# Probabilities turned by a bounce through DRAM, with ctx's blocks in four transfers, other PSUM banks and orders, and buffers on 512 bytes

## The chip, the cores and the metric

One core of one Trainium2 chip runs the whole program. The metric is the device time of the program in microseconds; the span of the profile, from the first instruction to the last, is some 2 us shorter. The kernel before was run three times: median 3147.73 us, 3147.18 to 3148.7.

## The reference, cut to what matters

64 items of 128 x 512 pass through two blocks. Block L0 is an attention over 512 positions with 128 channels and 1x1 convolutions; block L1 is a 16-head cross attention (head width 32, 128 queries, 128 keys) with an MLP of width 2048. All is float32.

```
# L0: x and ctx are (64, 128, 512); Wn, Wm, Wl, Wo are 128 x 128
Mn = Wn @ inorm(x) + bn ;  Mm = Wm @ inorm(ctx) + bm
A  = softmax(Mn^T Mm)                      # 512 x 512 for each item
x1 = Wo @ ((Wl @ ctx + bl) @ A^T) + bo + x
# L1
q = layer_norm(x1) @ q_w ; k = ctx @ k_w ; v = ctx @ v_w     # 16 heads of 32, biases left out here
attn = softmax(where(mask, q k^T / sqrt(32), min))
hidden = (attn @ v) @ cproj_w + cproj_b + x1
out = hidden + gelu(layer_norm(hidden) @ fc_w + fc_b) @ proj_w + proj_b
```

## The kernel before

The program is two passes. **attention_pass** computes `hidden` item by item and stores it in DRAM; **mlp_pass** reads it in 16 groups of four items and writes `out`. Float32 precision on TensorE comes from three passes: each operand is split into a high half of type float32r and the low rest, and a product is a_hi b_lo + a_lo b_hi + a_hi b_hi (`three_passes`). So each split operand needs a ScalarE or VectorE copy (hi) and a subtraction (lo).

In the first pass one item goes through five pipeline stages, one per **slot**. In slot s, b0 = item s does M, the 512 x 512 scores S0 and their exp into A; b1 = s-1 turns A (AT), computes u, x1 and k and v; b2 = s-2 normalises x1, computes q, the head scores S1, their row maxima (line 798) and the exps (line 618) into `probs`; b3 = s-3 normalises the probabilities on GpSimd (line 510), turns them on TensorE (line 936, 16 transposes of 128 x 128, evicted to `pT` on ScalarE, line 605), multiplies with v (PV, line 951), splits outT and starts cproj; b4 adds the residual into `hid` (line 700), which is stored. Slots 6 and on are a hardware loop of two slots (`slots`, `Item`). Each engine runs its own list of instructions strictly in the order written in its `slot` function and waits on semaphores; there is no planner. The orders of the five lists therefore set everything. All DMAs are issued by SyncE, whose `slot` stores hidden of b4, loads x and ctx of item s+2, the residual x and the mask, and then ctx's blocks for item s+1.

ctx is turned without TensorE: `load_blocks` brings the 32 x 32 blocks of an item into transposed block places in 16 transfers of 16 KB in pieces of 128 bytes, and one VectorE transpose (line 791), which turns each 32 x 32 block within itself, finishes the job. VectorE also scales A by the reciprocal sums (line 751) and makes the high halves of the normed inputs (line 778). The second pass turns its activations in the same manner, from SBUF into SBUF (`spread`, line 1096, and line 1220), for all groups but the first.

All SBUF tensors are allocated in the order of the code. `ident` fills 512 bytes of each partition and `neghalf` 16, so `stage`, `rows`, `y`, `first_hi` and `first_lo` behind them start 160 bytes past a multiple of 512. `rest_hi` and all that follows in the second pass starts 448 past one, and so do qc_hi, qc_lo and outT; ctxT, m and normed start 32 past, xnT 256 past. The split weights of k and v, and the first two weight stages of the MLP, share `first_hi` and `first_lo`.

## Time and profile before

| | |
|---|---|
| profiled execution | 3145.55 us, span 3143.7 us |
| median of the runs shown | 3147.73 us |
| first pass | to about 1724 us, 26.0 us an item in its loop |
| second pass | from about 1725 us, 16 groups |
| granted TensorE clock, mean | 0.994 |
| DMA packets | 342,417, of them 286,176 under 512 bytes |
| HBM | read 97.57 MB, written 33.55 MB |

The page gives each engine's busy time as a sum over the span. A matmul's duration in the trace overlaps the next one's: in a steady stream a long matmul (512 columns) lasts about 390 ns in the record while the next starts about 230 ns after it. The busy column is therefore the union of all.

### The profile page before, as it was taken

The numbers are of one execution on the slowest core, as the hardware profiler recorded it, in microseconds if no ns is written. First come the engines' busy times: TensorE is split into PE (matmuls) and PEld (weight loads), VectorE is DVE, ScalarE is ACT, GpSimd is POOL, SyncE is SP. The second block draws the span as 40 slices with busy tenths as digits, with TensorE's granted clock in tenths as the row PEclk, the third lists the DMA queues.
The fourth block names the chain that finished last, engine by engine and source line by source line (L and its number), as shares of the span: only waits on it lengthen the run. The fifth ranks groups of instructions, "written<-read, shape, count | busy, mean of one in ns | idle before, by whom it ended". The sixth has DMA issues, their size and how long they took to land. (4 is left out here: it accounts for less than half of the span.)

```text
span 3143.7 us, 56992 instructions
## 1 busy us (share of the span) xinstructions
PE 3091.3 (98%) x18551; PEld 2556.6 (81%) x18551; DVE 1952.3 (62%) x3961; ACT 1353.6 (43%) x3954; POOL 818.0 (26%) x742
## 2 busy tenths in 40 slices
PE   7999999999999999999997999999999999999999
PEld 5888888888888888888886788888888888888887
DVE  7888888888888888888885533333333333333332
ACT  4666666666666666666665311111111111111111
POOL 4444444444444444444443100000000000000000
PEclk9999999999999999999998999999999999999999
DMA  4111111111111111111112311111111111111110
GB/s 116 49 51 50 50 50 50 50 50 51 53 51 54 51 52 53 50 50 50 50 37 67 97 32 41 40 40 40 40 33 20 40 33 34 40 40 40 40 27 14
DMA packets 342417, 147.59 MB, mean 47 GB/s; under 512 B 286176, under 2 KB 286688, under 8 KB 342368
## 3 DMA queue, kind: packets, MB, share of 16 engines
q1 hardware_dynamic: 342368, 146.96, 17.6%
q8 instruction: 28, 0.46, 0.1%
q14 instruction: 21, 0.17, 0.0%
HBM read 97.57 MB, written 33.55 MB: 42 GB/s over the span
## 5 line engine op out<-in xcount | busy, mean ns | idle before, releaser
L1163 ACT ACTIVATE gl<-pre,fc_bias 128x512 f32<-128x512 f32 x256 | 176.6, 690 | 1127.9 <-PE pre L1248 1127.9
L1202 DVE CAST hT_hi<-gl 128x512 fp32r<-128x512 f32 x256 | 108.9, 426 | 847.5 <-ACT gl L1163 847.5
L618 ACT ACTIVATE rows<-bank,negmax 128x128 f32<-128x128 f32 x1024 | 362.9, 404 | 89.4 <-DVE negmax L798 89.4
L1247 PE MATMUL pre<-yT_hi,rest_lo 128*128 128x512 f32 x768 | 299.2, 390 | 0.0
L1246 PE MATMUL pre<-yT_lo,rest_hi 128*128 128x512 f32 x768 | 299.0, 389 | 0.0
L1248 PE MATMUL acc<-rest_hi,hT_hi 128*128 128x512 f32 x768 | 298.9, 389 | 0.0
L1248 PE MATMUL pre<-yT_hi,rest_hi 128*128 128x512 f32 x768 | 298.8, 389 | 0.0
L1246 PE MATMUL acc<-rest_lo,hT_hi 128*128 128x512 f32 x768 | 298.8, 389 | 0.0
L1247 PE MATMUL acc<-rest_hi,hT_lo 128*128 128x512 f32 x768 | 298.8, 389 | 0.0
L510 POOL TENSOR_TENSOR rows<-rows,rsum 128x512 f32<-128x512 f32 x256 | 258.8, 1042 | 18.8 <-DVE rsum L693 18.8
L862 PEld LDWEIGHTS bank<-ident,rows 128*128 128x128 f32 x2048 | 234.1, 142 | 22.4 <-ACT rows L618 3.7
L862 PE MATMUL bank<-ident,rows 128*128 128x128 f32 x2048 | 247.1, 274 | 4.2 <-ACT rows L618 3.3
L618 ACT ACTIVATION_READ_ACCUMULATOR rows<-bank,negmax 128x1 f32 x1024 | 249.2, 243 | 0.0
L154 POOL TENSOR_TENSOR rstd<-ve,neghalf 128x4 f32<-128x4 f32 x16 | 16.3, 1019 | 888.3 <-DVE ve L148 888.3
L589 ACT ACTIVATE rows<-bank,negmax 128x512 f32<-128x512 f32 x256 | 173.5, 685 | 122.7 <-DVE negmax L721 122.7
L831 PE MATMUL bank<-first_lo,ctxT_hi 128*128 128x512 f32 x512 | 214.1, 418 | 0.0
L833 PE MATMUL bank<-first_hi,ctxT_hi 128*128 128x512 f32 x512 | 203.0, 397 | 0.0
L832 PE MATMUL bank<-first_hi,ctxT_lo 128*128 128x512 f32 x512 | 202.5, 395 | 0.0
L535 POOL TENSOR_TENSOR normed_lo<-normed,normed_hi 128x512 fp32r<-128x512 f32 x128 | 180.4, 1431 | 50.1 <-DVE normed_hi L778 50.1
L1204 DVE TENSOR_TENSOR hT_lo<-gl,hT_hi 128x512 fp32r<-128x512 f32 x256 | 177.3, 693 | 8.8
L1246 PEld LDWEIGHTS pre<-yT_lo,rest_hi 128*128 128x128 f32 x768 | 144.2, 188 | 30.5
L1248 PEld LDWEIGHTS pre<-yT_hi,rest_hi 128*128 128x128 f32 x768 | 144.2, 188 | 30.3
(158 smaller groups left out, 7277.8 us busy)
## 6 DMA issues: line engine op xcount, KB each, us to landing
x_in<-in_x SPq DMA_DIRECT2D x64, 256.0 KB, 2.7
ctx_in<-in_ctx SPq DMA_DIRECT2D x64, 256.0 KB, 2.9
blocks<-in_ctx SPq DMA_DIRECT2D x1024, 16.0 KB, 2.0
small<-in_x SPq DMA_DIRECT2D x64, 256.0 KB, 3.3
hidden<-hid SPq DMA_DIRECT2D x64, 256.0 KB, 2.1
rows<-hidden SPq DMA_DIRECT2D x16, 1024.0 KB, 5.6
out<-rows SPq DMA_DIRECT2D x64, 256.0 KB, 2.1
stage<-y SPq DMA_DIRECT2D x240, 64.0 KB, 2.3
```

The lines of the kernel that those rows point to most:

```text
L510: pool.tensor_tensor(probs[:, r, :, :], probs[:, r, :, :], rsum1[:, r, :].unsqueeze(2).to_broadcast([P, 4, P]), ALU.mult).then_inc(probs_s ...
L535: pool.tensor_tensor(normed_lo[:, i, :], normed[:, i, :], normed_hi[:, i, :].bitcast(F32), ALU.subtract).then_inc(normed_lo_set, 1)
L618: act.activation(probs[:, r, c, :], by_chunk(S1_BANK[r])[:, c, :], ACT.Exp, bias=negmax1[:, r, c:c + 1], accum_out=sum1[:, r, c:c + 1]).th ...
L831: pe.matmul(out, a_hi, b_lo, start=first, stop=False)
L832: pe.matmul(out, a_lo, b_hi, start=False, stop=False)
L833: return pe.matmul(out, a_hi, b_hi, start=False, stop=last)
L862: last = pe.transpose(out[:, c * P:(c + 1) * P], src(c), ident[:])
L1163: act.activation(gl[:, i % 2, :], pre[i % 2][:], ACT.Gelu_apprx_tanh, bias=mlp.fc_bias[:, i:i + 1]).then_inc(gelu_done, 1)
L1204: dve.tensor_tensor(hT_lo[:, i % 2, :], gl[:, i % 2, :], hT_hi[:, i % 2, :].bitcast(F32), ALU.subtract).then_inc(hT_lo_set, 1)
L1246: pe.matmul(out, a_hi, b_lo, start=first, stop=False)
L1247: pe.matmul(out, a_lo, b_hi, start=False, stop=False)
L1248: return pe.matmul(out, a_hi, b_hi, start=False, stop=last)
```

## The change

- The probabilities are no longer turned on TensorE. GpSimd normalises them one slot earlier (for b2, in four pieces between other work). At the start of the next slot SyncE writes them to a DRAM scratch `p_turn` in four transfers, whose source is in pieces of 32 elements (`write_probs`), and reads them back in four transfers of 32 partitions each with rows of 2 KB (`read_probs`) into `p_blocks`, which lies in the weights' staging buffer. Four VectorE transposes of 32 x 32 blocks then write `pT`. The ScalarE evictions (line 605) and the 16 TensorE turns (line 936) are gone.
- ctx's blocks come in four transfers with 512-byte pieces in place of 16, and VectorE turns them with strided access patterns, earlier in its slot. The resulting order of ctx's columns is permuted. It is matched by the order in which the k and v weights are staged and by a permuted column order in which the exp writes A.
- ScalarE takes over the scaling of A and the high halves of the normed inputs.
- PSUM banks are assigned anew, and the orders on all engines change: cproj of an item is computed one slot later, behind M; TensorE does the head scores before PV, and PV waits for the VectorE turns; the k turn comes before V. VectorE adds `hid` after m_lo.
- Small tensors are allocated first with a pad or last, so that all large buffers start on multiples of 512 bytes.
- The MLP's weight stages swap halves of the staging buffer (`half_of`), and its second stage is loaded two slots later.

```diff
+        sb("pad", [P, PAD])
...
+        p_blocks = stage[:, 0, :, :]
+        p_turn = nc.dram_tensor("p_turn", [4, P, T], F32, kind="Internal").ap()
...
-        M_BANK = (5, 6)
-        AT_BANK = (4, 0, 1, 7)
...
+        M_BANK = (4, 7)
+        C_BANK = PV_BANK = 5
+        AT_BANK = S1_BANK = (0, 1, 2, 3)
...
# SyncE
-                    for c in range(4):
-                        sp.dma_start(to[32 * d:32 * (d + 1), :, c, :], of[:, :, c, d, :]).then_inc(blocks_in, 16)
+                    sp.dma_start(to[32 * d:32 * (d + 1), :, :], of[:, :, d * P:(d + 1) * P]).then_inc(blocks_in, 16)
...
+            def write_probs(e):
+                after(probs_set, e.nth(4, 4))
+                for d in range(4):
+                    sp.dma_start(p_turn[d].rearrange("p (h b) -> p h b", b=32),
+                                 mlp.rows[:, 1, :, :].rearrange("p r (c d b) -> p d (r c) b", d=4, b=32)[:, d])\
+                      .then_inc(p_written, 16)
+
+            def read_probs(e):
+                if e.has_before(1):
+                    after(pT_set, (e + -1).nth(4, 4))
...
+                after(p_written, e.nth(64, 64))
+                for d in range(4):
+                    sp.dma_start(p_blocks[32 * d:32 * (d + 1), :, :],
+                                 p_turn[d].rearrange("(q p) n -> p q n", p=32)).then_inc(p_blocks_in, 16)
+
             def slot(s):
-                e = s + -4
-                if e.exists():
-                    after(hid_set, e.nth(1, 1))
-                    sp.dma_start(hidden[e.number], hid[:, e.parity, :]).then_inc(hid_stored[e.parity], 16)
+                if (s + -3).exists():
+                    write_probs(s + -3)
...
+                e = s + -4
+                if e.exists():
+                    after(hid_set, e.nth(1, 1))
+                    sp.dma_start(hidden[e.number], hid[:, e.parity, :]).then_inc(hid_stored[e.parity], 16)
+                if (s + -3).exists():
+                    read_probs(s + -3)
...
# GpSimd
+                normalise(0)
+                normalise(1)
                 if b0.exists():
                     pool.wait_ge(ctxT_hi_set, b0.nth(1, 1))
...
+                normalise(2)
+                normalise(3)
# ScalarE
-                if b3.exists():
-                    for r in range(4):
-                        act.wait_ge(pT_turned, b3.nth(4, r + 1))
-                        act.activation(pT[:, r, :, :].rearrange("p c n -> p (c n)"), bank[PT_BANK[r]][:],
-                                       ACT.Copy).then_inc(pT_copied, 1)
+                if b0.exists():
+                    act.wait_ge(rsum0_set, b0.nth(1, 1))
+                    for t in range(DC):
+                        act.activation(A[:, t, :], A[:, t, :], ACT.Identity,
+                                       scale=rsum0[:, t:t + 1]).then_inc(a_scaled, 1)
...
+                if ahead.exists():
+                    for i in range(2):
+                        act.wait_ge(normed_set, ahead.nth(2, i + 1))
+                        act.activation(normed_hi[:, i, :], normed[:, i, :], ACT.Copy).then_inc(normed_hi_set, 1)
...
+                if b2.exists() and b2.has_before(1):
+                    act.wait_ge(p_written, b3.nth(64, 64))
                 exp1(0)
                 exp1(1)
+                if b3.exists():
+                    act.wait_ge(outT_done, b3.nth(1, 1))
+                    act.activation(flat(outT_hi), bank[PV_BANK][:], ACT.Copy).then_inc(outT_hi_set, 1)
+                exp1(2)
...
                 exp1(3)
# VectorE, behind qT and x1n
-                if b3.exists():
-                    dve.wait_ge(outT_hi_set, b3.nth(1, 1))
-                    lower(flat(outT_lo), bank[PV_BANK][:], flat(outT_hi), outT_lo_set)
+                if b3.exists():
+                    dve.wait_ge(p_blocks_in, b3.nth(64, 64))
+                    for r in range(4):
+                        dve.transpose(pT[:, r, :, :].rearrange("p c (q b) -> p c q b", b=32),
+                                      p_blocks[:, :, r * P:(r + 1) * P].rearrange("p q (c b) -> p c q b", b=32))\
+                           .then_inc(pT_set, 1)
                 if b2.exists():
                     dve.wait_ge(s1_done, b2.nth(1, 1))
...
# TensorE; S1, ahead of this, stood behind PV
+                if b3.exists():
+                    pe.wait_ge(pT_set, b3.nth(4, 4))
...
```

## Rows read from the trace of the kernel before

**Rows 1.** The page, part 1: busy us (share of the span) and instructions, by engine.

```profile
PE 3091.3 (98%) x18551; PEld 2556.6 (81%) x18551; DVE 1952.3 (62%) x3961; ACT 1353.6 (43%) x3954; POOL 818.0 (26%) x742
```

**Rows 2.** Stages, window by window: columns PE, PEld, DVE, ACT, POOL, PEclk, DMA share, GB/s.

```profile
500.00:1000.00 500.00, 500.00 (x3694) 416.92 (x3694) 425.95 (x888) 330.17 (x1074) 206.73 (x191) 1.00 0.19 51
```

**Rows 3.** Timeline of PE in one slot: start, us, engine, line, operation, tiles, count.

```profile
1000.00 1.91 PE L862 MATMUL bank<-ident,rows 128*128 128x128 f32 x16
1001.74 0.60 PE L862 MATMUL bank<-ident,x1n 128*128 128x128 f32 x4
...
1005.07 1.08 PE L951 MATMUL bank<-y,v_sb 128*32 128x128 f32 x32
...
1007.30 0.50 PE L831 MATMUL bank<-first_lo,ctxT_hi 128*128 128x512 f32 x1
...
1025.77 0.39 PE L833 MATMUL bank<-u_hi,small_hi 128*128 128x512 f32 x1
```

**Rows 4.** Groups by line, second pass: after the count busy us, mean ns of one.

```profile
L1248 PE MATMUL acc<-rest_hi,hT_hi 128*128 128x512 f32 x595 | 231.5, 389 | 0.0
...
L1248 PE MATMUL acc<-first_hi,hT_hi 128*128 128x512 f32 x208 | 82.3, 396 | 0.0
```

**Rows 5.** Groups by line, PE, first pass, 1000 to 1200 us.

```profile
L833 PE MATMUL bank<-first_hi,ctxT_hi 128*128 128x512 f32 x64 | 25.3, 396 | 0.0
...
L833 PE MATMUL bank<-qc_hi,outT_hi 128*128 128x512 f32 x32 | 12.5, 390 | 0.0
...
L833 PE MATMUL bank<-qc_hi,xnT_hi 128*128 128x512 f32 x28 | 11.1, 395 | 0.0
...
L832 PE MATMUL bank<-normed_hi,small_lo 128*128 128x512 f32 x16 | 6.4, 399 | 0.0
```

**Rows 6.** Timeline from one slot's row maxima to the next's, DVE and ACT.

```profile
1007.46 2.48 DVE L798 TENSOR_REDUCE negmax<-bank 128x4 f32<-128x512 f32 x4
...
1008.18 0.37 ACT L618 ACTIVATE rows<-bank,negmax 128x128 f32<-128x128 f32 x1 [1.36 <-DVE negmax L798]
...
1014.27 1.40 ACT L571 ACTIVATE m_hi<-bank,bias 128x512 fp32r<-128x512 f32 x2
...
1033.46 2.48 DVE L798 TENSOR_REDUCE negmax<-bank 128x4 f32<-128x512 f32 x4
```

**Rows 7.** Timeline of POOL, the end of a slot.

```profile
1011.68 1.29 POOL L541 TENSOR_TENSOR ctxT_lo<-small_t,ctxT_hi 128x512 fp32r<-128x512 f32 x1 [4.90 <-ACT ctxT_hi L628]
1012.93 4.04 POOL L510 TENSOR_TENSOR rows<-rows,rsum 128x512 f32<-128x512 f32 x4
```

**Rows 8.** Tile stage, 1795 to 1820 us: durations min/median/max, first and last start.

```profile
L1096 SPq DMA_DIRECT2D stage<-y x16: 624/632/1643, 1799.0 to 1810.2; - x16
L1220 DVE STREAM_TRANSPOSE y<-stage x4: 670/672/715, 1812.3 to 1814.1; 128x512 f32<-128x512 f32 x4
```

**Rows 9.** Stages: inside the second pass's bounce (columns as Rows 2).

```profile
1801.00:1808.00 7.00, 7.00 (x33) 5.79 (x31) 2.20 (x4) 1.10 (x2) 0.00 (x0) 1.00 0.63 99
```

**Rows 10.** DMA issues: count, KB each, median us from issue to landing.

```profile
blocks<-in_ctx SPq DMA_DIRECT2D x1024, 16.0 KB, 2.0
...
rows<-hidden SPq DMA_DIRECT2D x16, 1024.0 KB, 5.6
```

**Rows 11.** Timeline of DVE from x1 to the turn of ctx's blocks.

```profile
1026.50 0.75 DVE L758 SCALAR_TENSOR_TENSOR x<-bank,out_bias,small 128x512 f32<-128x512 f32 x1
...
1029.46 0.76 DVE L778 CAST normed_hi<-normed 128x512 fp32r<-128x512 f32 x2
...
1031.58 0.70 DVE L791 STREAM_TRANSPOSE small_t<-blocks 128x512 f32<-128x512 f32 x1
```

**Rows 12.** Timeline of the first pass's last two row maxima and PV, DVE and PE.

```profile
1681.72 2.48 DVE L798 TENSOR_REDUCE negmax<-bank 128x4 f32<-128x512 f32 x4
...
1697.74 2.48 DVE L798 TENSOR_REDUCE negmax<-bank 128x4 f32<-128x512 f32 x4
...
1708.43 1.08 PE L951 MATMUL bank<-y,v_sb 128*32 128x128 f32 x32 [0.69 <-ACT y L605]
```

More of the change, by code:

```diff
@@ L483, in load_for_mlp, with load_second_for_mlp @@
                              allow_slow_non_contiguous=True).then_inc(mlp.vecs_in, 16)
-                for n in range(2):
-                    sp.dma_start(stage[:, n, :, :], mlp_stage_source(w, n)).then_inc(mlp.staged[n], 16)
-            slots(sp, slot, {B + 1: load_for_mlp})
+                sp.dma_start(stage[:, half_of(0), :, :],
+                             mlp_stage_source(w, 0)).then_inc(mlp.staged[half_of(0)], 16)
+            def load_second_for_mlp():
+                sp.wait_ge(pT_set, 4 * B)
+                sp.dma_start(stage[:, half_of(1), :, :],
+                             mlp_stage_source(w, 1)).then_inc(mlp.staged[half_of(1)], 16)
+            slots(sp, slot, {B + 1: load_for_mlp, B + 3: load_second_for_mlp})
         @block.gpsimd
@@ L693, in sum1_reciprocal @@
                         dve.reciprocal(rsum1[:, r, :], sum1[:, r, :]).then_inc(rsum1_set, 1)
+                sum1_reciprocal(b3, 3)
+                if b0.exists():
+                    for i, b in enumerate(M_BANK):
+                        dve.wait_ge(m_hi_set, b0.nth(2, i + 1))
+                        dve.scalar_tensor_tensor(out=m_lo[:, i, :], in0=bank[b][:], scalar=bias0[:, i:i + 1],
+                                                 in1=m_hi[:, i, :].bitcast(F32), op0=ALU.add,
+                                                 op1=ALU.subtract).then_inc(m_lo_set, 1)
                 if b4.exists():
@@ L775, in slot @@
                                           in_rstd[:, i:i + 1], ALU.subtract, ALU.mult).then_inc(normed_set, 1)
-                    for i in range(2):
-                        dve.wait_ge(normed_set, ahead.nth(2, i + 1))
-                        dve.tensor_copy(normed_hi[:, i, :], normed[:, i, :]).then_inc(normed_hi_set, 1)
                 if b2.exists():
@@ L929, in slot @@
                         .then_inc(out0_done, 1)
-                if b3.exists():
-                    pe.wait_ge(exp1_done, b3.nth(16, 16))
-                    for r in range(4):
-                        pe.wait_ge(probs_set, b3.nth(4, r + 1))
-                        if r >= 2 and b0.exists():
-                            pe.wait_ge(exp0_done, b0.nth(4, r - 1))
-                        turn(bank[PT_BANK[r]], lambda c: probs[:, r, c, :], pT_turned)
                 if b2.exists():
@@ L943, in slot @@
                     if b0.exists():
[L944 removed]
+                        pe.wait_ge(exp0_done, b0.nth(4, 1))
                     project(bank[K_BANK], ctxT_hi, ctxT_lo, K_W, k_done)
[L946 to L954 removed]
                 if b2.exists():
@@ L973, in slot @@
                     mm.then_inc(s1_done, 1)
+                if b3.exists():
+                    pe.wait_ge(pT_set, b3.nth(4, 4))
+                    for c in range(4):
+                        for r in range(4):
+                            h = 4 * c + r
+                            mm = pe.matmul(bank[PV_BANK][32 * r:32 * r + 32, c * P:(c + 1) * P],
+                                           v_sb[:, b3.parity, h * HD:(h + 1) * HD], pT[:, r, c, :],
+                                           start=True, stop=True)
+                    mm.then_inc(outT_done, 1)
                 if b1.exists():
+                    pe.wait_ge(k_copied, b1.nth(1, 1))
+                    turn(bank[KT_BANK], lambda c: k_sb[:, c * P:(c + 1) * P], kT_turned)
                     if not b1.has_before(1):
```

233 lines of the change are left out of this document (110 added, 123 removed).

## The prediction, made before the change was run

> **What bounds the kernel now.** I read the page's busy shares and slices first. TensorE is busy 3091 of the span's 3143.7 us; VectorE, the next that computes, 1952 [rows 1]. The profiled execution took 3145.55 us; the median of the runs shown is 2.2 us above it, so I sum against the trace and add 2.2. The stage table then shows the first pass: in 500 us TensorE is busy for all 500, VectorE 426, ScalarE 330, GpSimd 207, the granted clock is 1.00 (the 2.4 GHz level), and the DMA share is 0.19 [rows 2]. The timeline gives the period of one slot: the row maxima of the scores (line 798) start at 1007.46 and again at 1033.46, so 26.0 us per batch item [rows 6]. TensorE has no gap there. Yet VectorE has only 4 us of idle time in a slot, and its order is fixed, so a TensorE that does less is not by itself a shorter slot. What matters is which round trips from one row maximum to the next are nearly 26 us long. That decides this case.
>
> **TensorE's saving.** The 16 turns of the probabilities start at 1000.00, and the next turns at 1001.74: 1.74 us [rows 3]. With a switch between kinds of matmul saved (0.1) that is 1.85 us. The alignment: in the second pass nothing differs between weights in the handover's buffers and in later ones but the address, and their matmuls last 395 to 396 against 389 ns [rows 4]. In the first pass the same mark is on ctxT, xnT and normed (394 to 399), not on outT (390) [rows 5]. Buffers on 512 bytes should bring all to 389: some 50 of the 81 long matmuls of a slot by 5 to 8 ns, 0.35 to 0.4 us a slot; in the second pass 96 matmuls a group by 6.5 ns, 0.63 us times 16 groups, 10 us. TensorE alone would need 26.0 - 1.85 - 0.4 = 23.75 us a slot.
>
> **What the bounce puts in its place.** The new order makes a ring through one slot. Call 0 the start of the row maxima, right behind the four new VectorE turns.
> - Exp: the first starts 0.72 after the maxima, and the 16 heads with m_hi behind them take until 1014.27 in the trace, ctxT_hi (0.5) among them: 0.35 us a head [rows 6]. The new order puts outT_hi (another 0.5) behind head group 1 and ctxT_hi behind group 2. Group 2 ends at 0.72 + 12 x 0.345 + 0.5 = 5.4, ctxT_hi at 6.1.
> - GpSimd: ctxT_lo 1.29, then the normalisations of groups 2 and 3, 1.01 each (four in 4.04) [rows 7]: 6.1 + 1.3 + 2.0 = 9.5, the probabilities complete. The last group's exp ends at 7.4, so GpSimd decides.
> - The bounce itself, from there to p_blocks landed. Out: 1 MB in 128-byte pieces, 8192 of them, four issues. The nearest rows are the second pass's bounce, SBUF to SBUF, also 8192 pieces of 128 bytes: first issue 1798.99, VectorE could start at 1812.3, so 13.3 us [rows 8], at 99 GB/s and a DMA share of 0.63 [rows 9]. It is issued in 16 parts over 11.2 us, 0.75 each, which is what keeps the share low; 99 / 0.63 = 157 GB/s gives 6.7 us, and 1.6 to 2.0 of start and landing (2.0 for a 16 KB transfer [rows 10]) make 8.5. Back: 1 MB in 2 KB pieces, 5.6 as rows<-hidden [rows 10], but SyncE now issues x_in, ctx_in, x_res and hidden between them, 1 MB that lies in the same queue ahead of it. Low for the whole bounce: pieces at the 2 KB rate both ways, 5.6 + 0.3 + 5.6 = 11.5. High: 13.3 out, 0.3 for the wait, 5.6 and 0.2 of queue, 19.4. At 157 GB/s it is 8.5 + 0.3 + 5.6 = 14.4, or with the loads ahead 15.5. I take 15.3: the issues are four, so it should be nearer to the fabric's rate than to 13.3 out.
> - Four VectorE turns: 2.5 us (0.70 for one turn of that size [rows 11], the next starts 0.1 before its end) and 0.1 to notice the landing.
> Sum: 9.5 + 15.3 + 2.6 = 27.4 us a slot. By the ends: 23.6 and 31.5.
>
> **A second ring, through TensorE and VectorE.** The PV products wait for the turned probabilities. Behind them stand, in order, k's turn, V, M, cproj, the turns, S0, U, Q and out0; x1 waits for out0; and VectorE reaches the probabilities' turns only behind x1. In the trace PV starts at 1005.07 and out0 ends at 1025.77 + 0.39 = 1026.16: 21.1, less the scores' matmuls now ahead of PV (PV ends at 1006.15, V starts at 1007.30: 1.2) and 0.4 of alignment: 19.5 [rows 3]. x1 to the slot's own turn is 1026.50 to 1031.58, less the casts that leave VectorE (0.7): 4.4 [rows 11]. With the new turns (2.5): 19.5 + 4.4 + 2.5 = 26.4, with nothing of the DMA in it. So even a perfect bounce doesn't shorten the slot.
>
> **The other edits of VectorE and ScalarE.** VectorE loses the scaling of A (1.6) and two casts (0.7), and gains 2.5 of turns [rows 11]: no change. ScalarE loses the four copies of turned probabilities and gains the four scalings and two casts, each an instruction over 512 elements like them: two more in a slot in which it is busy for 17 of 26 us [rows 2]. They stand ahead of the exps, where it has waited for the row maxima, and cost nothing; without that idle time they would push the exps back by up to 1.2 us. The column order of A's exp is a permutation: nothing. ctx's blocks: 16 issues become four, which frees the issuing queue; that is needed, as SyncE now waits twice within a slot. Behind its wait for the written probabilities stand only the reads and the next ctx blocks, which nobody needs for half a slot.
>
> **Ends of the pass.** The drain has no other work to hide the bounce. The last two row maxima start at 1681.72 and 1697.74 and the last PV at 1708.43, intervals of 16.0 and 10.7 [rows 12]. Without the loads in the queue the bounce is 14.4. The first interval becomes 9.0 + 14.4 + 2.6, some 25.5 to 26 (nearer 25.5, as fewer exps stand between); the second, without ctxT, 0.7 + 5.5 of exps + 1.2 of normalising + 14.4 + 2.6 = 24.4. That is 9.5 + 13.7 = +23 us. The second weight stage of the second pass is loaded two slots later, behind the last turns, and is needed only at the first proj: nothing, at most 5 us.
>
> **Sum.** 62 intervals x (27.4 - 26.0) = +87; ends +23; second pass -10; total +100. 3145.55 + 100 + 2.2 = **3248 us**.
>
> **A rule of the skill.** The rows show 128-byte pieces into SBUF only, at 157 GB/s of full share [rows 9]; none shows them into DRAM. The Trainium skill, "DMA: Bandwidth & Descriptors", Specifications, gives 512 bytes as the least transfer for line rate and says that below it the engine reads, modifies and writes. By that rule the way out would be near or past my high end; it is the mechanism named by the third rival. No row bears it out or refutes it.
>
> **The rivals.**
> 1. The bounce is hidden (under about 14.4 us) and the second ring sets 26.4: 62 x 0.4 + 23 - 10 = +38, 3186 us. For: rows<-hidden's 5.6 for 1 MB. Against: the loads in the queue ahead of the reads. Chance 0.20.
> 2. The other side: TensorE stays the bound, with 23.75 a slot, because VectorE's waits in the second ring are slack that closes (four idle us per slot [rows 2], part of them spent waiting for TensorE) and the bounce lasts under 11.6. Then 62 x -2.25 = -140, ends +20, second pass -10: -130, 3018 us. It decides from the ring through x1: that must shrink by 0.4 us for steady slots as long as before, by 0.7 for a kernel faster by more than 0.2% against the drain's cost, and by 2.65 for the full gain. For: TensorE is the only engine without a gap. Against: the order of the waits as summed. Chance 0.18 for anything faster.
> 3. Pieces into DRAM are slower than into SBUF: bounce 19.4 or more, 31.5 a slot, 62 x 5.5 + 35 - 10 = +366, 3514 us. Then TensorE stands still for 8 us a slot. For: nothing in the trace writes small pieces into DRAM. Against: the low price of small pieces elsewhere. Chance 0.10.
> 4. The change saves as much as it costs (within 6 us of 3147.7; 0.2%, about what a measurement of this kernel can tell from no change): 0.05.
> My forecast, the bounce's ring between 26.5 and 30 us, holds the remaining 0.47. Its own range is 3195 to 3400. The range for 8 in 10 leaves out most of the faster case and of rival 3: 3130 to 3400. Faster 0.18, same 0.05, slower 0.77.
>
> **What would show it.** In the profile after, the stage table over 500 us must show TensorE under 450 busy with the wait in front of PV (released by VectorE's turns), and VectorE's wait in front of the turns released by the DMA into the blocks: 1 to 4 us a slot. If that DMA wait is absent but the slot is 26.4, it is rival 1. The period of the row maxima tells the case at a glance. Matmuls with the handover's weights must fall to 389 ns; if they don't, the 10 us and the 0.4 a slot are gone. Against the forecast would be a TensorE without gaps, or a bounce that lands in under 14 us. The write's time to landing (8.5 taken) and the read's (5.6) stand in the list of DMA issues.

## The result, and the profile after

The changed kernel takes 3390.14 us, the kernel before 3147.61: a ratio of 1.0776, 95% interval 1.0732 to 1.082, 242 us slower. The forecast had the sign, and its range held the time, but it gave the change +100, less than half of its effect. The profiled execution (3380.77 us, span 3378.9) is the shortest of four, the longest took 3407.72; the stretches below are the profiled one's, and their sum is 7 us short of the 242.

The additions to kT, one a slot, and the first turn of the second pass cut the span. First before, then after: durations, first and last start.

```profile
L809 DVE TENSOR_TENSOR kT<-bank,vecs x64: 659/660/680, 49.8 to 1685.5; 128x512 f32<-128x512 f32 x64
```

```profile
L859 DVE TENSOR_TENSOR kT<-bank,vecs x64: 657/660/691, 50.0 to 1882.7; 128x512 f32<-128x512 f32 x64
...
L1289 PE MATMUL tr<-ident,y x16: 421/421/476, 1947.9 to 1951.5; 128*128 128x128 f32 x16
```

The second pass starts at 1724.7 in the trace of before. So:

| stretch | before | after | difference | forecast |
|---|---|---|---|---|
| 63 slots | 1635.7 | 1832.7 | +197.0 | +87, for 62 |
| drain of the first pass | 39.2 | 65.2 | +26.0 | +23 |
| second pass | 1419.0 | 1431.0 | +12.0 | -10 |

In the middle of the first pass (48 slots, from the 9th addition to kT) a slot went from 26.01 to 29.21 us. All slots below are measured so.

The page, part 1 [rows 1], and the stages [rows 2]: TensorE has gaps in both passes, and in the first its mean granted clock is below 1.

```profile
PE 3080.9 (91%) x17527; PEld 2521.7 (75%) x17527; DVE 1934.2 (57%) x3833; ACT 1442.4 (43%) x4082; POOL 788.9 (23%) x742
```

```profile
500.00:1000.00 500.00, 441.89 (x3004) 359.85 (x3003) 369.62 (x742) 314.74 (x984) 176.23 (x169) 0.92 0.59 115
...
2000.00:2500.00 500.00, 494.48 (x2178) 408.29 (x2177) 185.94 (x355) 85.16 (x123) 35.88 (x29) 1.00 0.15 41
```

Waits from 500 to 1500 us (us in total, times, longest). The two forecast waits are there: PV for VectorE's turns, and the turns for the read from DRAM.

```profile
PE bank L1025 <- DVE y L847: 88.6, 34, 3.9
...
DVE y L847 <- DMA stage<-p_turn: 42.4, 34, 2.5
```

One slot of TensorE, VectorE and SyncE (start, us; answers to [rows 3, 6, 11]). PV waits 2.94 us. The same matmuls into v's bank that last 0.39 elsewhere then last 0.63.

```profile
1035.30 0.40 PE L1012 MATMUL bank<-mask_less,masked_bf 1*128 1x512 bf16 x4 [0.71 <-DVE qT L838]
1035.51 1.07 PE L1017 MATMUL bank<-kT,qT 32*128 32x128 f32 x32
1039.52 1.08 PE L1025 MATMUL bank<-y,v_sb 128*32 128x128 f32 x32 [2.94 <-DVE y L847]
1040.54 1.08 PE L920 MATMUL bank<-ident,k_sb 128*128 128x128 f32 x4
...
1042.26 0.63 PE L891 MATMUL bank<-first_hi,ctxT_hi 128*128 128x512 f32 x1
```

```profile
1034.87 0.53 DVE L842 TENSOR_SCALAR x1n<-x,x_mv,x_rstd 128x512 f32<-128x512 f32 x1
1036.98 2.49 DVE L847 STREAM_TRANSPOSE y<-stage 128x512 f32<-128x512 f32 x4 [1.58 <-DMA stage<-p_turn]
1039.39 2.45 DVE L853 TENSOR_REDUCE negmax<-bank 128x4 f32<-128x512 f32 x4
```

```profile
1020.16 4.32 SPq L457 DMA_DIRECT2D p_turn<-rows  x4
1024.85 1.20 SPq L413 DMA_DIRECT2D x_in<-in_x  x1
...
1028.50 0.37 SPq L499 DMA_DIRECT2D hidden<-hid  x1
1029.12 1.78 SPq L469 DMA_DIRECT2D stage<-p_turn  x4
```

The granted clock by stretches of 3 us (columns as [rows 2]): 1.00 through the gap's start, 0.60 right behind it, that is mostly the level of 1.2 GHz.

```profile
1037.00:1040.00 3.00, 0.48 (x19) 0.48 (x22) 3.00 (x6) 0.00 (x0) 1.31 (x2) 1.00 0.00 0
1040.00:1043.00 3.00, 3.00 (x32) 2.51 (x22) 1.92 (x5) 2.86 (x17) 1.00 (x1) 0.60 0.00 0
```

DMA issues (KB each, median us to landing), answering [rows 10]:

```profile
p_turn<-rows SPq DMA_DIRECT2D x256, 256.0 KB, 4.7
stage<-p_turn SPq DMA_DIRECT2D x256, 256.0 KB, 4.8
```

The drain [rows 12]: PV waits 8.92 and 15.42 us there.

```profile
1905.70 1.93 PE L1025 MATMUL bank<-y,v_sb 128*32 128x128 f32 x32 [8.92 <-DVE y L847]
1930.74 1.93 PE L1025 MATMUL bank<-y,v_sb 128*32 128x128 f32 x32 [15.42 <-DVE y L847]
```

The second pass. The handover's weights are now at 389 ns as the rest [rows 4], but TensorE stands still, for "issue", that is, it waits for nothing that the profile shows:

```profile
L1295 PE MATMUL acc<-rest_hi,hT_hi 128*128 128x512 f32 x763 | 296.9, 389 | 0.0
L1295 PE MATMUL acc<-first_hi,hT_hi 128*128 128x512 f32 x256 | 99.6, 389 | 0.0
```

```profile
2219.98 0.49 PE L1293 MATMUL pre<-yT_lo,first_hi 128*128 128x512 f32 x1 [0.44 <-issue]
...
2223.27 0.51 PE L1293 MATMUL pre<-yT_lo,first_hi 128*128 128x512 f32 x1 [2.34 <-issue]
```

Such a stretch comes once in each turn of the second pass's hardware loop, every 177 us. The queue of instruction fetches moved 81 pieces of 16 KB, and 28 in the kernel before. So each pass has a loss for which the forecast has no term: the clock behind PV's wait, and these stalls.

### The profile page after: what moved, and what is told of

It reads as the page before. It is cut to its first block and busy times, and to the rows that moved or that the text cites. A ratio compares the mean times of both kernels' runs of the same rounds, so it can differ in the third digit from the quotient of the medians.

```text
span 3378.9 us, 53422 instructions
## 1 busy us (share of the span) xinstructions
PE 3080.9 (91%) x17527; PEld 2521.7 (75%) x17527; DVE 1934.2 (57%) x3833; ACT 1442.4 (43%) x4082; POOL 788.9 (23%) x742
## 3 DMA queue, kind: packets, MB, share of 16 engines
q8 instruction: 81, 1.33, 0.2%
## 5 line engine op out<-in xcount | busy, mean ns | idle before, releaser
L1025 PE MATMUL bank<-y,v_sb 128*32 128x128 f32 x2048 | 104.6, 369 | 185.0 <-DVE y L847 185.0
L889 PE MATMUL bank<-first_lo,ctxT_hi 128*128 128x512 f32 x512 | 236.8, 462 | 0.0
L669 ACT ACTIVATION_READ_ACCUMULATOR rows<-bank,negmax 128x1 f32 x1024 | 235.9, 230 | 0.0
L1025 PEld LDWEIGHTS bank<-y,v_sb 128*32 128x32 f32 x2048 | 75.5, 146 | 201.3 <-DVE y L847 181.7
L890 PE MATMUL bank<-first_hi,ctxT_lo 128*128 128x512 f32 x512 | 217.2, 424 | 0.0
L891 PE MATMUL bank<-first_hi,ctxT_hi 128*128 128x512 f32 x512 | 214.2, 418 | 0.0
L847 DVE STREAM_TRANSPOSE y<-stage 128x512 f32<-128x512 f32 x256 | 159.4, 680 | 95.6 <-DMA stage<-p_turn 95.6
L579 POOL TENSOR_TENSOR normed_lo<-normed,normed_hi 128x512 fp32r<-128x512 f32 x128 | 160.0, 1272 | 120.0 <-ACT normed_hi L663 120.0
L741 DVE TENSOR_TENSOR at_lo<-bank,at_hi 128x512 fp32r<-128x512 f32 x256 | 159.0, 683 | 17.1 <-ACT at_hi L626 17.1
```

Of the source, the lines that this page charges most:

```text
L669: act.activation(probs[:, r, c, :], by_chunk(S1_BANK[r])[:, c, :], ACT.Exp, bias=negmax1[:, r, c:c + 1], accum_out=sum1[:, r, c:c + 1]).th ...
L889: pe.matmul(out, a_hi, b_lo, start=first, stop=False)
L890: pe.matmul(out, a_lo, b_hi, start=False, stop=False)
L891: return pe.matmul(out, a_hi, b_hi, start=False, stop=last)
L1025: mm = pe.matmul(bank[PV_BANK][32 * r:32 * r + 32, c * P:(c + 1) * P], v_sb[:, b3.parity, h * HD:(h + 1) * HD], pT[:, r, c, :], start=True ...
```

## The experiments

| kernel | us | ratio to before, 95% | slot | second pass |
|---|---|---|---|---|
| no bounce | 3238.94 | 1.0289 (1.0272 to 1.0306) | 27.30 | 1433 |
| read into 128 partitions | 3331.84 | 1.0593 (1.0576 to 1.0611) | 28.16 | 1431 |
| write in 2 KB | 3254.25 | 1.0342 (1.0324 to 1.0359) | 27.32 | 1433 |
| loads behind the read | 3277.31 | 1.0406 (1.0389 to 1.0424) | 27.30 | 1432 |
| fillers | 3299.60 | 1.0485 (1.0468 to 1.0503) | 28.21 | 1408 |
| no bounce, fillers | 3168.95 | 1.0067 (1.0051 to 1.0084) | 26.54 | 1409 |
| changed, 102 waits | 3380.56 | 1.0734 (1.0716 to 1.0752) | 29.79 | 1408 |
| before, 154 waits | 3148.38 | 1.0000 (0.9991 to 1.0010) | 26.01 | 1419 |
| before, 80 matmuls | 3167.98 | 1.0061 (1.0044 to 1.0078) | 26.01 | 1419 |
| before, 39 matmuls | 3178.28 | 1.0098 (1.0081 to 1.0115) | 26.01 | 1445 |
| before, aligned | 3121.32 | 0.9911 (0.9895 to 0.9928) | 25.75 | 1408 |
| the same, ctx in four | 3120.87 | 0.9914 (0.9897 to 0.9930) | 25.77 | 1408 |
| turn first, no DRAM | 3470.11 | 1.1023 (1.1003 to 1.1043) | 30.70 | 1428 |
| late PV, 1 to 5 | 3297.05, 3254.52, 3208.64, 3185.19, 3181.51 | 1.0474 to 1.0110 | 28.25, 27.61, 26.84, 26.38, 26.39 | 1404 to 1408 |

**The bounce taken away.**

```diff
-                if (s + -3).exists():
-                    write_probs(s + -3)
-                    read_probs(s + -3)
...
-                    act.wait_ge(p_written, b3.nth(64, 64))
+                    act.wait_ge(pT_set, b3.nth(4, 4))
...
-                    dve.wait_ge(p_blocks_in, b3.nth(64, 64))
+                    dve.wait_ge(probs_set, b3.nth(4, 4))
```

> The changed kernel without its eight transfers of the probabilities: nothing is written to p_turn and nothing read back, VectorE's four turns wait for the normalised probabilities alone and turn what lies in the staging buffer (so the values of ctx's attention are left out). Theory: the slot of 29.2 us is the ring row maxima, exponentials, normalisation (10.3), bounce (16.5), turns (2.5). Without the bounce that ring is 13 us and the next one sets the slot, the one through out0, x1, k and V, forecast at 26.4: 62 x (29.2 - 26.4) = 174 us less, 3216. Rival A: TensorE's own work is next, 23.75 a slot: 3390 - 62 x 5.45 = 3052. Rival B: the slot is long because TensorE's clock and the new order of its work make it so, and the bounce waits for that: under 30 us less, 3360 or more.

The bounce costs 151 us, no more: 1.91 of the 3.20 us by which the slot grew. What is left, 27.30, is nearest to the expected 26.4. TensorE's waits from 500 to 1500 us:

```profile
PE bank L1021 <- DVE y L843: 46.6, 37, 1.3
PE bank L1008 <- DVE qT L834: 26.6, 37, 0.7
```

PV still waits 1.3 us, now only because VectorE's turns (2.5 us) stand behind qT and x1n. By microseconds, the granted clock behind that gap:

```profile
1023.00:1024.00 1.00, 0.11 (x4) 0.00 (x0) 1.00 (x3) 0.00 (x0) 1.00 (x2) 0.99 0.93 334
1024.00:1025.00 1.00, 0.62 (x12) 0.59 (x16) 1.00 (x3) 0.00 (x1) 0.84 (x1) 0.50 0.54 179
...
1027.00:1028.00 1.00, 1.00 (x6) 0.88 (x5) 0.06 (x1) 1.00 (x7) 0.90 (x1) 0.81 0.00 0
```

That doesn't happen in every slot. Behind the same gap, PV runs at full speed in one slot and at half speed in another:

```profile
560.45 1.08 PE L1021 MATMUL bank<-y,v_sb 128*32 128x128 f32 x32 [1.24 <-DVE y L843]
1024.38 1.93 PE L1021 MATMUL bank<-y,v_sb 128*32 128x128 f32 x32 [1.27 <-DVE y L843]
```

Of 36 slots from 500 to 1500 us, measured from PV to PV, 14 are of the first kind and last 26.55 us on the average, 22 are of the second and last 27.78. What decides between them no run shows. The 26.55 is the second ring as forecast (26.4): 19.86 from PV to the end of out0 (19.5 forecast), 4.15 from there to VectorE's turns (4.4), 2.54 for the turns (2.5). The clock's fall makes the first part 21.10, and changes nothing else.

**The cold clock.** Fillers are long matmuls whose result nobody reads. They keep TensorE busy where it would wait, and go into a bank that is free there; 3 and 10 of them in the changed kernel, 3 and 5 without the bounce.

```diff
+            def fill(n):
+                for _ in range(n):
+                    pe.matmul(bank[KT_BANK][:], m_hi[:, 0, 0:P], m_hi[:, 1, :], start=True, stop=True)
+                        fill(3)                      # ahead of the scores
+                        fill(10)                     # ahead of PV
```

> The changed kernel with 3 long matmuls that nobody reads ahead of the scores and 10 ahead of PV, into a bank that is free there (13 x 0.227 = 3.0 us, where TensorE has gaps of 0.7 and 1.6 to 4.3 us). Theory: the granted clock falls to 0.50 after the gap ahead of PV and stays there for 3 to 4 us, so PV, the turns of k and the projection to V run at half speed and V ends 1.7 us late; the upper half of ctx, the lower half and two normalisations wait for V, 0.8 us of which lie on the ring through the bounce. The clock stays up, V's matmuls start 227 ns apart again, the slot falls by 0.8 to 1.0 us, the whole by some 55 to 3335. Rival: the ring doesn't pass through V (VectorE's and ScalarE's own queues set the normalisation's time): 3380 to 3400.

> The changed kernel without its eight transfers of the probabilities (3239), and with 3 long matmuls that nobody reads ahead of the scores and 5 ahead of PV (1.8 us, where TensorE has gaps of 0.7 and 1.3 us in each slot). Theory: the 1.3 us that its slot of 27.3 is longer than the 26.0 of the kernel before come from the clock: it falls to 0.50 after the gap of 1.3 us and costs 1.9 us in the 3.8 us that follow. With the gaps filled the slot is 27.3 - 1.8 = 25.5 or a little less: 3239 - 62 x 1.8 = 3127. Rival: the gaps themselves and the chain behind them (out0, x1, x1n, turns, PV) set the slot: the fillers change nothing, 3239, or cost up to 62 x 0.5 us.

In the changed kernel useless work made the kernel 90 us faster: 1.0 us a slot, and 23 us of the second pass (below). The mean clock of the middle is back at 1.00. Measured from the row maxima, V's last matmul ended at 6.13 in the changed kernel and at 4.58 with the fillers, the probabilities were normalised at 10.32 and 9.39. That is the ring, through V and ctxT: in the changed kernel ctxT's upper half waits for V in 29 of 34 slots (from 500 to 1500 us):

```profile
ACT ctxT_hi L685 <- PE bank L891: 31.6, 29, 2.0
```

Without the bounce the fillers gave 0.76 us, not 1.8. TensorE is then full (499.57 of 500); its own work, the 2.22 us of fillers taken off, is 26.54 - 2.22 = 24.3 us a slot. The fillers don't set that slot: it is the second ring's, the 26.55 of the slots above in which the clock stayed up without them.

```profile
500.00:1000.00 500.00, 499.57 (x3498) 399.73 (x3497) 406.72 (x830) 346.72 (x1082) 196.45 (x188) 1.00 0.15 50
```

**The parts of the bounce.** Into all partitions, from 2 KB pieces, and with nothing between write and read:

```diff
-                    sp.dma_start(p_blocks[32 * d:32 * (d + 1), :, :],
-                                 p_turn[d].rearrange("(q p) n -> p q n", p=32)).then_inc(p_blocks_in, 16)
+                    sp.dma_start(p_blocks[:, d, :], p_turn[d]).then_inc(p_blocks_in, 16)
```

> The changed kernel, with each of the four transfers back from DRAM going into all 128 partitions (2 KB each) and not into 32 (four of 2 KB each): the same bytes, the same size of piece and the same number of pieces, but the turned values are then out of place (that part of the result is left out). Theory: the pieces into 32 partitions took 139 ns and ran at 235 GB/s, half of what a transfer over 128 partitions reaches, so the data's 5.5 us become about 2.8: the ring is 2.7 us shorter, 26.5 a slot, 62 x 2.7 = 167 us less, 3223. Rival: the way back costs its issue and its latency (4 x 1.2 + 2 us), and the rate hides beneath: under 0.7 us a slot, 3350 or more.

```diff
-                    sp.dma_start(p_turn[d].rearrange("p (h b) -> p h b", b=32),
-                                 mlp.rows[:, 1, :, :].rearrange("p r (c d b) -> p d (r c) b", d=4, b=32)[:, d])\
+                    sp.dma_start(p_turn[d], mlp.rows[:, 1, d, :])\
```

> The changed kernel with each of the four transfers to DRAM written as 128 rows of 2 KB and not as 2,048 pieces of 128 bytes: the same 1 MB, the probabilities then come back out of place (that part of the result is left out). Theory: the 8,192 pieces of 128 bytes took 6.1 us at 1,350 in a us, and their four issues 1.2 us each; 512 pieces of 2 KB need some 3 us and issue in under 2, so the ring through the bounce falls by over 3 us, to under 26. Then the slot is that of the kernel without the bounce, 27.3: 62 x 1.9 = 118 us less, 3272, and with the tail's share 3255. Rival: what is waited for is mostly the fixed part from issue to landing, and the loads that stand between the write and the read: under 0.5 us a slot, 3360 or more.

```diff
 # SyncE, slot s
-   write_probs; load x_in, ctx_in; load x_res, mask; store hidden; read_probs; load_blocks
+   load x_res, mask; write_probs; read_probs; load x_in, ctx_in; store hidden; load_blocks
```

> The changed kernel with SyncE's order changed: the loads of x_in and ctx_in and the store of hidden stand behind the read of the probabilities, x_res and the mask ahead of their write, so that nothing lies between write and read. The whole result is computed. Theory: 0.75 MB less in the queue between the two and four issues less; the read starts some 1.1 us sooner, the slot falls to 28.1, 62 x 1.1 = 68 us, 3322. Rival: the read is issued when the last of the 8,192 pieces has landed, the loads only fill that time, and the slot stays within 0.3 us: 3375 or more.

The wide read gave 1.05 us a slot (2.7 expected), the big pieces 1.89, the order of the queue 1.91. The last two land on the slot without a bounce, 27.30: either of them hides it, and the changed kernel was some 2 us over an edge. Landing of write and read, first 2 KB pieces, then the other order, which puts no transfer's bytes ahead of the read (with the wide read it is 3.9):

```profile
p_turn<-rows SPq DMA_DIRECT2D x148, 256.0 KB, 2.3
stage<-p_turn SPq DMA_DIRECT2D x144, 256.0 KB, 5.1
```

```profile
p_turn<-rows SPq DMA_DIRECT2D x148, 256.0 KB, 4.6
stage<-p_turn SPq DMA_DIRECT2D x148, 256.0 KB, 4.2
```

In the latter VectorE waits for the read in 6 of 37 slots, 1.6 us in all, and TensorE's waits are those of the kernel without a bounce:

```profile
PE bank L1024 <- DVE y L846: 48.1, 36, 1.7
...
DVE y L846 <- DMA stage<-p_turn: 1.6, 6, 0.4
```

The rival of the loads' run, a read gated by the last piece's landing, fell: the read is issued 7.95 us after the write's first issue and not 9.0, and takes 0.7 less to land. In the changed kernel the write has landed after 7.9 us; SyncE then still issues the loads and the store, without a pause, for another 1.1 us before it comes to the read. x_in's issue alone takes 1.20 us right behind the write's, and 0.36 in the other order.

**The second pass.** Waits, then matmuls of one column, between the passes, to move the loop's instructions:

```diff
             slots(pe, slot, {0: prepare_small})
+            for _ in range(102):          # changed; 154 in the kernel before
+                pe.wait_ge(small_turned, 3)
```

```diff
+            for _ in range(39):           # before; 80 in the first try
+                pe.matmul(bank[6][:, 0:1], ident[:], ident[:, 0:1], start=True, stop=True)
```

> The changed kernel with 102 satisfied waits added to TensorE's instructions between its passes, where it waits for the first group's rows anyway: the second pass's loop then lies where it did before in blocks of 256 instructions. Theory: the stalls of 2.2 to 2.5 us in TensorE, about two for each turn of the second pass's loop, with instruction fetches beside them, come from where the loop lies; they go, the second pass falls from 1431 to about 1409 us, the whole to 3368. Rival: they come from something else in the second pass (the buffers' new places, the DMA of weights): 3390, the stalls remain.

> The kernel before, with 154 satisfied waits added to TensorE's instructions between the passes, where it waits for the first group's rows: the second pass's loop then lies in blocks of 256 instructions as it does in the changed kernel. Theory: the stalls of the changed kernel's second pass come from that place alone, so they show up here too, two of 2.2 to 2.5 us and the instruction fetches for each turn of the loop, and the second pass grows from 1419 by some 23 us: 3171. Rival: the loop's place doesn't matter, and what changed in the run with 102 waits was something else: 3148 to 3156 (154 waits are a few us at the most, in a gap).

> The kernel before with 80 matmuls of one column, read by nobody, added between the passes (TensorE waits there). Two waits in a row make one instruction, so the 154 waits of the last try moved the loop by 77 instructions only; in the traces the last instruction fetch of a turn of the loop came 1,086 matmuls after the second pass's start (before), 1,107 (102 waits), 1,042 (154 waits), all without stalls, and 1,132 in all five kernels that stall, 36 matmuls ahead of the loop's end. 80 matmuls bring it to about 1,134. Theory: the place of the loop alone makes the stalls: the second pass grows from 1419 to 1442, the whole to 3171, and about 80 instruction fetches stand in the trace. Rival: the stalls belong to something else in the changed kernel: 3148 to 3155.

> The kernel before with 39 float32 matmuls of one column between the passes. The 80 of the last try moved the loop by about 326 instructions (the last fetch of a turn at 1,049), four for each and not two; 39 move it by some 159 and bring that fetch to about 1,132, where it stands in all kernels that stall. Theory: 12 to 14 stalls of 2.2 to 2.5 us, some 80 fetches, the second pass 1442 for 1419; with some 10 us for the 39 matmuls themselves 3180. Rival: the second pass stays at 1419, and the whole at 3158.

With 102 waits the changed kernel's second pass has no gap and takes 1408.3; the run's total fell by 10 only, as its first pass was slower (slots of 29.2 to 29.8 occur in one and the same order). In the kernel before, 154 waits did nothing, and 80 matmuls took 21 us between the passes and left the second pass at 1419.4. A total of 3168 that lay next to the expected 3171 was chance: the second pass itself and the fetches had to be looked at. The traces say why. Between two fetches in a row TensorE runs some 256 instructions (246 to 271 in the kernel before, matmuls and weight loads counted apart); 102 waits appear as 51 instructions and 154 as 77; and a float32 matmul of one column appears as four, two loads and two matmuls. Counted from the second pass's start, the last fetch of the loop's first turn comes after 1,086 matmuls (before), 1,107 (102 waits), 1,042, 1,049 (80 matmuls), all quiet, and after 1,131 to 1,134 in the six kernels with the changed kernel's code length, all stalling. 39 matmuls bring it to 1,132 in the kernel before, and there it stalls:

```profile
q8 instruction: 83, 1.36, 0.2%
```

```profile
PE pre L1250 <- issue: 14.1, 6, 2.5
PE pre L1248 <- issue: 2.3, 5, 0.6
```

1444.9 for 1419.0, +26 us, by code that isn't in the loop. The Trainium skill, "Runtime: NRT & Kernel Launch", Instruction fetch mechanics, has blocks of 16 KB or 256 instructions, room for 2048 instructions for TensorE, and a stall where a taken branch's target is not held; the size of the fetches agrees. Why just this place stalls, with a loop of 1,582 instructions, no run shows.

**The alignment and ctx's blocks, alone.**

```diff
+        sb("pad", [P, PAD])
+        self.ident = sb("ident", [P, P])     # and all large buffers behind it
```

> The kernel before with nothing changed but the places of its buffers: the small ones together, and all the large ones on a multiple of 512 bytes. Theory: that alone makes long matmuls start 226.6 to 227 ns apart, where they are 231 to 237 apart before; the second pass, which TensorE fills, falls by 2 per cent, some 25 us (in the changed kernel it did so but for the stalls), and the first pass, which is set by a ring with TensorE's work in it, by 62 x 0.2 = 12 us: 3110. Rival: the spacing comes with the banks or the order of the changed kernel and not with the places: 3148.

```diff
-                    for c in range(4):
-                        sp.dma_start(to[32 * d:32 * (d + 1), :, c, :], of[:, :, c, d, :]).then_inc(blocks_in, 16)
+                    sp.dma_start(to[32 * d:32 * (d + 1), :, :], of[:, :, d * P:(d + 1) * P]).then_inc(blocks_in, 16)
```

> The kernel before with its buffers on 512 bytes (3121), and ctx's blocks in four transfers of 512-byte rows in place of sixteen of 128 bytes, with the keys, the rows of k's and v's weights and the exponentials' columns in the order that this gives. Theory: the sixteen transfers were hidden, TensorE is busy in every slot, and the strided output of the four exponentials costs nothing that is on a path: 3121, within 6 us. Rival A: SyncE's queue, relieved of twelve issues a slot, lands other loads sooner: 10 us or more faster. Rival B: the exponentials' strided output makes them longer and the ring through the row maxima with them: 10 us or more slower.

The places alone are worth 27 us: 10.9 of the second pass, where 25 were expected, and 0.26 a slot. The four transfers are worth nothing. These are the two fastest kernels here. Not all places off 512 were slow: in the kernel before `rest_hi` and outT, 448 bytes past a multiple, ran at 389 and 390 as well; 160, 32 and 256 past were the slow ones. Which offsets are good no run maps.

**Another way round.** VectorE turns first and sixteen transfers of 2 KB rows go from SBUF to SBUF.

```diff
-    write_probs(e); read_probs(e)            # 4 + 4 through DRAM
+                for g in range(4):
+                    for j in range(4):
+                        sp.dma_start(mlp.y[32 * j:32 * (j + 1), g, :],
+                                     p_blocks[32 * g:32 * (g + 1), j, :]).then_inc(pT_in, 16)
```

> A version that keeps the idea and drops the bounce: VectorE turns the blocks of 32 x 32 first, inside SBUF, with an output order that puts the 16 heads' parts for one group of 32 keys side by side (2 KB); sixteen transfers of 32 rows of 2 KB then move them from SBUF to SBUF, with no DRAM between; VectorE's turns stand right after the first attention's row maxima, qT ahead of the next item's normalisation, PV behind the turns of k. The whole result is computed. Theory: the bounce's price was its small pieces (8,192 of 128 bytes, 6.1 us) and the cold clock behind PV's wait. Here the probabilities are turned some 7 us ahead of PV, sixteen issues of 0.35 us and about 2 us of landing fit, no gap of over 1 us is left and TensorE's own work sets the slot: 24.3 us (the slot of the run with fillers, 26.54, less its 2.2 of fillers). First pass 1714 - 62 x 1.4 = 1627, whole 3121 - 87 = 3034; up to 3060 with small gaps. Rival: sixteen issues and the half rate into 32 partitions take over 9 us, PV waits, the clock falls, and the slot is 27 or more: 3190 or more.

I had priced an issue at 0.35 us, from the loads of ctx's blocks. These take 0.59, and one follows another after 0.63; each 32 rows of 2 KB. Sixteen need 10 us, and PV waits, 3.6 us in this slot, as the rival had it:

```profile
L459 SPq DMA_DIRECT2D y<-stage x16: 562/590/600, 1010.8 to 1020.3; - x16
...
  PE bank L1021: 3.6, 1
```

**PV a slot later.** The bounce stays as it is; all five have the 102 waits.

```diff
 # VectorE
-   x1n; turns of the probabilities; row maxima; ...; kT; outT_lo; rsum(2); v_sb
+   x1n; row maxima; kT; turns; ...; rsum(2) | v_sb, outT_lo in the next slot     # 1: turns behind rsum(2)
+   qT ahead of normed                                                           # from 3
+   v_sb ahead of m_lo                                                           # from 4
 # TensorE
-   M; output projection; turns of A; turns of x1n; ...; scores; PV; turns of k; V
+   M; PV; turns of A; turns of x1n; output projection; ...; scores; turns of k; V
+   PV behind two of the four turns of A                                         # 5
```

> The changed kernel with the bounce as it is, but PV read later: VectorE's four turns stand behind the second attention's row maxima and the addition to k, PV opens TensorE's next slot behind the first projections, v's bias is added behind PV, the output projection follows the turns of x1n, and TensorE has 102 waits between the passes that take the loop of the second pass off the place where it stalls. The whole result is computed. Theory: from the exponentials' row maxima to the turns the bounce then has a whole slot and 4.5 us; it ends with 1 to 4 us to spare, PV waits for nothing, the clock stays up, and TensorE's own work with the 0.7 us ahead of the scores sets the slot: 24.3 + 0.7 = 25.0 to 25.4. First pass 1948 - 62 x 4.0 = 1700, second 1408: 3110, under the kernel with aligned buffers (3121). Rival: the chain stays closed (maxima, exponentials, normalisation, bounce, turns, v's addition, maxima of the next slot) and the slot is 27 or more: 3230.

> The version with the late PV, and now kT's addition and VectorE's four turns right behind the second attention's row maxima, ahead of the reciprocals of the sums. The whole result is computed. Its forerunner's slot of 28.25 us had TensorE waiting 1.33 us for kT and 1.51 us for the turns, which stood behind a reciprocal that waits for the exponentials; the bounce had long landed. Theory: the bounce costs nothing once its turns don't stand ahead of the row maxima; both gaps go, the slot is TensorE's own work and 0.7 us: 25.2 to 25.5, 3297 - 62 x 2.9 = 3117 (3105 to 3135). Rival: the reciprocals, 2.5 us later, hold up the normalisation, the bounce and the turns, and the ring closes again at 27 or more: 3220.

> The same, and qT's addition ahead of the next item's two normalisations on VectorE. The whole result is computed. Theory: the gap of 0.7 us ahead of the scores goes, the slot is TensorE's own work, 24.4 to 24.8: 62 x 0.7 = 43 us under the run beside it, some 3075. Rival: the normalisations, 0.6 us later, hold up the first projections of the next slot, and the slot stays as it is beside it.

> The last version, with v's addition ahead of the lower halves of the first projections on VectorE. The whole result is computed. Theory: the turns of x1n no longer wait 1.2 to 1.5 us, the slot falls from 26.84 to 25.5: 3209 - 62 x 1.3 = 3128 (3120 to 3145). Rival: VectorE's own queue sets the slot, and the wait moves to the row maxima: 3190 or more.

> The same, and two of the first attention's four turned banks ahead of PV on TensorE, where it waits 0.84 us. The whole result is computed. Theory: TensorE is busy throughout, with its own 24.4 to 24.7 us: 62 x 0.8 = 50 us under the run beside it, some 3080, and the first kernel that beats the one with aligned buffers (3121). Rival: v's addition and all behind it come 0.9 us later, and nothing is gained on the run beside it.

None reached its expected time, though the third's step on the second (46 us for 43) came as forecast. In every one the read had landed before the turns (0.3 us before in the tightest slot): the bounce is free at a slot of 26.4 as well. Yet of most gaps removed only a part came back: kT's 1.33 and half of PV's 1.51 gave 0.64, qT's 0.71 all of it, 1.3 of x1n's turns gave 0.46, the rest of PV's (0.67) nothing. Each time the next wait for VectorE opened, in the last one that of the output projection:

```profile
PE bank L891 <- DVE outT_lo L741: 45.4, 38, 1.2
```

From the row maxima to outT_lo VectorE works in a fixed order with 1.4 us of waiting for exponentials in it, and the bounce's 2.5 us of turns lie in the middle. None reached TensorE's 24.3, and the drain is 61 to 63 us in all, 22 to 24 above before.

## Why the prediction was right in sign and short in size

The mechanism was right: the bounce closes a ring through one slot, PV waits for VectorE's turns, and they wait for the read. The step that failed is the sum of that ring, 27.4 us forecast and 29.2 measured, by two terms: "9.5 to the normalised probabilities", which has no term for TensorE's clock behind PV's wait (10.3), and "the bounce 15.3" (16.5). A third term, "second pass -10", measured +12. In the profiled execution 110 us of the miss lie in the slots, 22 in the second pass and 3 in the ends; the other 7 are the distance from the shortest execution to the median.

- **"TensorE alone 23.75"**: 24.3 measured with the fillers off. Alignment brought all long matmuls of the second pass to 389, as forecast. In the first, with the places alone changed, those of keys, values, L0's scores and the output projection still start 229 to 233 ns apart on the average and the others 227; a slot gains 0.26 and not 0.4. 25.75 less the 1.74 of the turns would be 24.0; the rest, switches between small and long matmuls of about 0.1 each among it, no run takes apart.
- **"9.5 to the normalised probabilities"**: 10.32. The order was right to the instruction; V ended 1.5 us late, at half clock. The sum lets ctxT's upper half follow the exponentials at 5.4 and has no term for V, for which that half waits: at 4.6, with the clock up, V would indeed have been in time, and the trace of before, in which TensorE never rests [rows 2, 3], shows nothing else. A forecast wait of 1 to 4 us in front of PV should have been followed by the question what TensorE's clock does behind it. With the clock held (fillers) the term is 9.39.
- **"The bounce 15.3"**: 16.5. Out: 9.0 from first write issue to first read issue, against 8.5 + 0.3. That the two agree is in part luck: the write landed after 7.9, well sized from the second pass's bounce [rows 8, 9], and the other 1.1 went to SyncE's issues, which this sum has at nothing. Back: 7.4 for 5.6. I took rows<-hidden's 5.6 for 1 MB [rows 10], which goes into 128 partitions, while each transfer here goes into 32, and I let the loads in the queue cost 1.1 at most. The pieces into 32 partitions took 139 ns on the average, and about 104 with the wide read, which landed 0.7 us sooner; with nothing between write and read it landed 0.7 sooner too.
- **"VectorE's turns 2.6"**: 2.5.
- Sum of the ring: 27.4 forecast, 29.2 measured; 62 x 1.8 = 112 of the 142 us missing. The fillers gave back 1.0 of it, the order of the queue 1.9.
- **"A second ring, 26.4"**, the floor under a bounce in this order: 27.3 on the average. The mechanism is right (PV behind the turns, the turns behind x1, x1 behind V and U), and the three kernels whose bounce is gone or hidden all stop there. Its size was right too where the clock stayed up, 26.55; the rest of the miss is the clock, which costs 1.2 us in 22 of 36 slots.
- **"Ends +23"**: +26. Right.
- **"Second pass -10"**: the -10.9 of the alignment came, and +22.7 of instruction fetches on top. I had no such term: nothing in the diff touches that pass's loop. It is 22 us of the miss.
- **Rival 3 (small pieces into DRAM)** is refuted: 8,192 pieces of 128 bytes took 6.1 us, 173 GB/s, where the sum had 157 for such pieces into SBUF, from 99 GB/s at a share of 0.63 [rows 9]. The Trainium skill, "DMA: Bandwidth & Descriptors", Specifications, has 512 bytes as the least transfer for line rate, with a read, modify and write below it. The prediction put the way out near or past 13.3 us by that; it took 7.9 to landing, so this trace doesn't bear it out at that size. Bigger pieces do land sooner (2.3 for 4.7 us) and issue in 1.8 for 4.3 us. **Rival 2 (TensorE the bound)** was out of reach in any order tried. **Rival 1 (hidden)** is what another order of the queue makes of it, with the whole result computed: a slot of 27.30 in place of its 26.4, for the clock.

## What to carry to other kernels

A wait that you add in front of the busiest engine costs more than its length: where the granted clock falls behind it (here the work of the next 3 to 4 us ran at half speed), add what that costs, and ask which ring that work is in. Size each transfer of a bounce by rows with the same number of partitions, and put nothing of the same queue between its two halves that can go elsewhere. After any edit that changes the number of instructions look at a hardware loop that it doesn't touch, for gaps "issue" and fetches; and read the stretch, not the total, when a total agrees.

## What was not expected of the hardware

- In the kernel without a bounce a gap of 1.3 us, with one of 0.7 us a little before it, brought the granted clock to 0.50 for 3 to 4 us in 22 of 36 slots, and left it at 1.00 in the other 14; in the first of the late-PV kernels gaps of 1.33 and 1.51 us with 1.4 us of long matmuls between them left it at 1.00 in all.
- The address of a buffer moves a long float32r matmul from 395 to 389 ns (second pass, 160 bytes past a multiple of 512 against none) and 27 us of 3147 in all, with no instruction changed.
- The place of a loop of 1,582 instructions costs 0 or 26 us of 1419.
- An issue of a 64 KB transfer on SyncE takes 0.59 us from SBUF to SBUF and 0.32 to 0.34 on the average from DRAM (ctx's blocks); one of 256 KB from SBUF to DRAM in 2,048 pieces of 128 bytes takes 1.05, and in 2 KB pieces 0.42.
